# Gated products of the FFN made two units at a time on GpSimd, and the copies of unit 11 moved ahead of the exponentials

## What is computed

```python
x = x + conv(ln_c(x))                  # q, k, v, beta; the delta rule in chunks of 16 tokens; Wo
t = tokens(x)
h = ln_t(t)
g = silu(einsum('bsd,edh->bseh', h, w_gate))
u = einsum('bsd,edh->bseh', h, w_up)
routed = einsum('bse,bsed->bsd', top2(softmax(h @ router_w)), einsum('bseh,ehd->bsed', g * u, w_down))
shared = silu(h @ ws_gate) * (h @ ws_up) @ ws_down
t = t + alpha * shared + (1 - alpha) * routed      # alpha = sigmoid(h @ sg_w + sg_b)
```

## Time and profile before

| what | value |
|---|---|
| median of three runs | 483.0 us |
| the profiled execution's own time | 483.11 us |
| its span, first to last instruction | 481.4 us |
| busy: PE / DVE / POOL / ACT | 86% / 88% / 84% / 72% |
| POOL `hid` L1007 | 192 instructions, 112.8 us |
| POOL waiting for ACT's `ug` | 18.4 us in 18 waits |
| granted TensorE clock, mean | 0.947 |

### The profile page before, as it was taken

The page is one execution under the profiler, slowest core; times in us unless marked ns, Lnnn a source line. Parts: engine busy times, 40 slices in busy tenths (PEclk is TensorE's granted clock), DMA queues, the critical chain, the costliest instruction groups (busy, mean ns, idle before and its releaser), DMA issues.

```text
span 481.4 us, 10362 instructions
## 1 busy us (share of the span) xinstructions
PE 415.3 (86%) x2400; PEld 384.0 (80%) x2400; DVE 421.3 (88%) x2270; ACT 344.5 (72%) x997; POOL 406.0 (84%) x519
## 2 busy tenths in 40 slices
PE   1344446999999999999999999999999989899996
PEld 0233325898999989998999999999999979798895
DVE  4689969999999999999999999999999999996200
ACT  3699546586978786877878686969695847475862
POOL 4366978899999999999999999999999999986340
PEclk9976555999999999999999999999999999999999
DMA  6555672623242223222232322322323232200301
GB/s 164 161 124 131 155 184 73 167 73 98 66 109 81 91 68 89 73 87 78 81 89 72 98 77 84 93 82 81 89 75 90 78 95 84 90 1 1 115 2 16
DMA packets 43437, 42.91 MB, mean 89 GB/s; under 512 B 20144, under 2 KB 35184, under 8 KB 43376
## 3 DMA queue, kind: packets, MB, share of 16 engines
q1 hardware_dynamic: 42768, 42.05, 32.5%
q10 hardware_dynamic: 608, 0.21, 0.2%
HBM read 35.95 MB, written 6.29 MB: 88 GB/s over the span
## 4 chain that ended last, share of the span: by engine, by line
DVE 60%; POOL 10%; PE 10%; issue 7%; ACT 1%; POOLq 0%; DVEq 0%; ACTq 0%
DVE Pr L1423 13%; DVE bank L1427 13%; DVE u L1425 12%; DVE SH L1431 11%; POOL PQ L969 3%; POOL PQ L962 3%; PE bank L463 2%; POOL hid L1007 2%; DVE otok L1236 1%; PE bank L436 1%; PE bank L448 1%; DVE ss L1204 1%; PE bank L440 1%; PE bank L438 1%; PE bank L439 1%
## 5 line engine op out<-in xcount | busy, mean ns | idle before, releaser
L1007 POOL TENSOR_TENSOR hid<-sg,ug 128x192 f32<-128x192 f32 x192 | 112.8, 606 | 22.0 <-ACT ug L714 18.4
L962 POOL TENSOR_TENSOR PQ<-SH,QB 128x768 f32<-128x768 f32 x62 | 112.6, 1838 | 0.7 <-DVE SH L1431 0.7
L713 ACT ACTIVATE sg<-bank 128x192 f32<-128x192 f32 x192 | 64.3, 335 | 61.5 <-PE bank L440 48.7
L969 POOL TENSOR_TENSOR PQ<-PQ 128x768 f32<-128x768 f32 (+2 forms) x93 | 102.9, 1106 | 6.1
L463 PE MATMUL bank<-Wd,hidT 128*128 128x192 f32 x576 | 106.6, 326 | 0.0
L1427 DVE TENSOR_TENSOR bank<-bank,u 128x96 f32<-128x96 f32 (+1 forms) x467 | 104.5, 265 | 0.5
L1425 DVE TENSOR_REDUCE u<-Pr 128x6 f32<-128x102 f32 (+1 forms) x437 | 102.5, 268 | 0.8 <-issue 0.3
L1423 DVE TENSOR_TENSOR Pr<-SH,bank 128x96 f32<-128x96 f32 (+1 forms) x437 | 101.0, 265 | 1.4
L1431 DVE TENSOR_TENSOR SH<-SH,bank 128x96 f32<-128x96 f32 (+1 forms) x467 | 101.9, 255 | 0.3
L463 PEld LDWEIGHTS bank<-Wd,hidT 128*128 128x128 f32 x576 | 94.4, 190 | 0.0
L436 PE MATMUL bank<-Whi,hiT 128*128 128x384 f32 (+1 forms) x192 | 73.0, 380 | 1.1 <-DVE loT L1166 1.1
(11 more groups left out here) (143 smaller groups left out, 814.2 us busy)
## 6 DMA issues: line engine op xcount, KB each, us to landing
QB<-q_scratch SPq DMA_DIRECT2D x64, 384.0 KB
k_scratch<-khl SPq DMA_DIRECT2D x64, 48.0 KB, 1.7
KR<-k_scratch SPq DMA_DIRECT2D x32, 96.0 KB, 2.4
q_scratch<-qn SPq DMA_DIRECT2D x64, 24.0 KB, 1.9
Wd<-in_L_ffn_w_down_dram SPq DMA_DIRECT2D x4, 288.0 KB, 8.2
out_dram<-xT SPq DMA_DIRECT2D x1, 896.0 KB, 4.1
Wlo_unsplit<-in_L_ffn_w_gate_dram SPq DMA_DIRECT2D x2, 384.0 KB, 4.4
Wlo_unsplit<-in_L_ffn_w_up_dram SPq DMA_DIRECT2D x2, 384.0 KB, 5.9
```

What stands on the lines that cost most here:

```text
L962: tt(PQ[:, at * BR * HP:(at + n) * BR * HP].rearrange("p (i b h) d -> p i b (h d)", i=n, b=BR), SH[:, lo:lo + n].rearrange("p i b h d -> p ...
L969: chained(tt(PQ[:, :, 0:w], PQ[:, :, 0:w], PQ[:, :, w:2 * w], ALU.add))
L1007: tt(hid[:, r * H:(r + 1) * H], sg[:, m % RING], ug[:, m % RING], ALU.mult).then_inc(s_hid, 1)
```

## The change

GpSimd's `hidden(m)` now makes units m and m+1 in one instruction of 384 columns: it waits for the copies of both, and raises `s_hid` by 2 when both are done. The list of GpSimd calls it for m = 0, 2, 4, 6, 8, 10. The pair (10, 11) stands ahead of the first reading's sums; before, unit 11 stood behind them. The pair (6, 7) stands behind `rs`; before, unit 6 stood ahead of it. The pair (0, 1) of chunk c-1 stands behind the second reading, its sums and `vn`; before, unit 0 stood ahead of the second reading. On ScalarE unit 11 is copied behind the second group of `hidT`, ahead of the output's copies and the exponentials; before, it stood behind them. The waits of ACT and PE are unchanged.

```diff
 # ScalarE
                     at(-2, unit, 10)
                     at(-2, hidden, 1)
+                    at(-2, unit, 11)
                     at(-3, Fc_out)
                     table(c + 2, LN_EXP)
...
                     table(0, SILU)
                     at(-2, hidden, 2)
-                    at(-2, unit, 11)
                     at(-1, unit, 0)
 # GpSimd
             def hidden(q, p, m):
-                pool.wait_ge(s_ug, q * UN + (m + 1))
+                pool.wait_ge(s_ug, q * UN + (m + 2))
...
-                    last = ((m - UN // 2) % UN + 1) * H - 1
+                    last = ((m + 1 - UN // 2) % UN + 1) * H - 1
...
-                r = m % (UN // 2)
-                tt(hid[:, r * H:(r + 1) * H], sg[:, m % RING], ug[:, m % RING], ALU.mult).then_inc(s_hid, 1)
+                r, s = m % (UN // 2), m % RING
+                tt(hid[:, r * H:(r + 2) * H].rearrange("p (m h) -> p m h", m=2), sg[:, s:s + 2], ug[:, s:s + 2],
+                   ALU.mult).then_inc(s_hid, 2)
...
-                    at(-2, hidden, 6)
                     if c <= NC:
                         rsqrt(c)
-                    at(-2, hidden, 7)
+                    at(-2, hidden, 6)
                     once(c, 1, weights_1, 10)
                     once(c, 1, weights_1, 11)
                     at(0, reading, 0)
                     at(-2, hidden, 8)
-                    at(-2, hidden, 9)
                     at(-2, hidden, 10)
                     at(0, summing, 0)
                     at(2, A_kn)
-                    at(-2, hidden, 11)
                     at(2, A_qn)
-                    at(-1, hidden, 0)
                     at(0, reading, 1)
                     at(0, summing, 1)
                     at(2, A_vn)
-                    at(-1, hidden, 1)
+                    at(-1, hidden, 0)
                     at(-1, hidden, 2)
-                    at(-1, hidden, 3)
                     at(-1, hidden, 4)
-                    at(-1, hidden, 5)
                     at(2, A_klo)
```

## The result

The changed kernel takes **526.5 us**, the median of six runs (524.9 to 530.5), against 483.1 us of the kernel before beside it. The ratio is 1.091, with an interval of 1.089 to 1.093. The forecast was 513 us with a range of 505 to 522: the direction is right, and the time lies 4.5 us above the range.

A forecast was written before the change was run, and what follows sets the result against it. DVE's recurrence was taken to set the 25.18 us turn; the change closes a loop of 27.5 us, 13 x 2.32 = 30.2 us more, so 483.1 + 30.2 = 513.3, forecast 513 us, range 505 to 522.

The forecast's parts named there:

- The mechanism: Pair (0, 1) behind the second reading holds ACT's unit 4 copy, then PE and DVE, in every turn: 2.3 us a turn.
- the sign: Expected waits: ACT at unit 4 50 us in all, DVE at two st some 2 a turn, GpSimd for ug over 40.
- The loop: GpSimd from (6, 7) to (0, 1), back over ACT and PE: 27.5 us a turn against 25.18.
- The stretch on GpSimd: From the start of (6, 7) to the end of (0, 1), pairs, readings and sums without a gap: 20.73 us.
- The way back: Unit 4's copy, PE's units 6 to 7, unit 7's copy and four handovers: 6.75 us.
- no worse than now: GpSimd's rs standing ahead of pair (6, 7): claimed no worse than before, given no cost.
- 292.08 to 297.34: 5.26: PE from the start of unit 6 to the end of unit 7: 5.26 us, a term of the loop.
- I leave both out: Two last turns may pay some tenths less, the steps behind them some tenths more; neither counted.
- Unit 11: Early copy on ACT, 0.5 to 0.6 us ahead of prob: costed at nothing; without the hold up to 0.1 a turn.
- GpSimd as the bound: Rival: GpSimd sets the pace and six pairs save 0.9 us a turn, giving 469 us; chance 0.03.
- The absorbed hold: Rival: ACT's stop at unit 4 replaces existing waits, the turn stays 25.18 and the time about 483 us; chance 0.04.
- The dear pair: Rival: a merged GpSimd pair is no cheaper than two single products, giving 522 us; chance 0.15.

The follow-up runs named there:

- the kept clock's kernel: The changed kernel with fourteen extra matmuls, whose results nobody reads, ahead of unit 6 on PE in each repeating step: 518.4 us, ratio 1.073.
- the six-slot kernel: The changed kernel with six slots for sg and ug instead of four (RING = 6), nothing else: 490.0 us, ratio 1.015.
- the last experiment: The kernel before with only the pairs (4, 5) and (8, 9) merged: 482.5 us against 482.9, ratio 0.999.

## Why the prediction was right, and where it was wrong

**The mechanism was right.** ACT stops at unit 4 (57.5 us in 14 times; the sign named 50), DVE stops at the two `st` (32.4 us more in 13 turns, 2.5 each; the sign named 2), GpSimd has no gap from (6, 7) to (0, 1), and the run that moves unit 0 alone gives 516 us. GpSimd's waits at the pairs are larger than named: 21.1 us put down to `ug` and 49.7 us to "issue". In the turn above, 2.98 us of these end when ACT has copied unit 5 (at 351.81 to 352.22 on its timeline): a pair waits for its second copy there. At (6, 7), which the sign named too, the pair itself waits for 0.1 us in this turn, since `rs` ahead of it has waited.

**The loop was right at full clock.** The stretch on GpSimd was summed to 20.73 us and measured 20.80; the pair was taken at 1.0 us and measured 1.01. The way back was summed to 6.75 and measured 6.97: 0.1 on PE, which starts its first matmul behind a pause with 0.44 us, and 0.1 in the handovers. That `rs` makes this no longer is luck: the forecast called it "no worse than now" and did not follow its way back, which in the turn shown ends within 0.01 us of unit 7's. With the clock kept up, 13 turns take 27.68 us each against 27.5.

**The step that failed is the way back, "292.08 to 297.34: 5.26", as the price of every turn.** It was read in a turn of before in which PE had not paused. The same loop makes PE wait 1.7 to 1.9 us right ahead of unit 6, and in some turns PE then runs at 0.50 of its clock through just this part of the loop: 6.89 us instead of 5.36 in the slow turn shown, and 8.38 in the first of the 13, behind a pause of 3.36. The forecast named the pause (unit 6 three us late) and gave it no price beyond its length. Kept busy, the kernel is 8.2 us faster; so that is the missing term, and without it 518.4 lies in the range.

**A second, smaller one:** "I leave both out", of the last turns and the steps behind them. At kept clock they cost 2.7 us (35.1 us in all, of which 13 turns make 32.4). The account is then 513.3 + 13 x 0.18 (turns) + 2.7 (ends) + 8.2 (clock) = 526.5 us. That the sum closes is no further proof: the clock term is the difference of two measured kernels, and the ends are what the kept clock's kernel leaves over.

**Unit 11** was costed at nothing under the hold and at up to 0.1 us a turn without it. Without it it costs 4.1 us in all; the forecast looked at `sel`, where it is indeed 0.12 us a turn, and not at `hidT` behind the exponentials. Under the hold the forecast's zero was not tried by itself.

**The rivals.** GpSimd as the bound is excluded: the two cheapest pairs save work there and no time. The absorbed hold is excluded by ACT's 57.5 us and the turns. The dear pair is excluded by its 1.01 us. What none of the rivals said is that a pair costs by what it makes wait, at both ends: unit 0 waits for unit 1's copy (1.5 us in the turn read ahead of the reading, where the kernel, with the rest of the change, is 31 us slower than before), and unit 2 is ready 0.4 us later (2.1 us of the kernel).

**Open** is how the 6.8 us that the six-slot kernel keeps divide. The early unit 11 makes 4.1 us alone and the pair (2, 3) 2.1 alone, and they don't simply add. The six-slot kernel's ordinary turn is that of the early unit 11 alone, 25.75 us against 25.76, with the same delays in the same places, and nothing of the pair is seen in it; the run that takes unit 11 back has almost the same turn with the loss in another place. Where the rest lies was not found, and what six slots would do to the kernel before was not run.

## What to carry to other kernels

Before a producer is moved behind long work or merged with its neighbour, ask which slot it frees and who stands in order behind the one that waits for the slot; if the way leads back to the producer, the delay is paid in every turn, and a deeper ring is the cheap remedy (36.5 of 43.4 us here, for two slots). A merged instruction starts at its last input and gives its first output at its end, so only neighbours whose first consumer has room should be merged, and only on an engine whose time counts. Where an edit gives TensorE a new pause, price the work behind it at both clocks: 1.5 us here in a turn in which the clock fell for 3.4 us.

## What the runs showed of the hardware

The length of PE's pause alone does not tell whether the clock falls. In the changed kernel's profile PE waited 1.74 us ahead of unit 6 at 319.76 and the clock fell to 0.50 for 3.4 us; 1.74 us at 264.24 and at 292.00 and 1.89 us at 349.20 left it at 1.00, with the same matmuls around them. Behind the last turn PE waits 3.34 us for unit 4 and the clock is at 0.50 for 6.8 us; that lies where the profiled execution lost 5.2 us. Filling the pause kept the clock up: fourteen matmuls that nobody reads, 1.81 us long together, in idle time, made the kernel 8 us faster.

The mean clock of a run has to be read with care. The three shortest runs of the changed kernel (524.9 to 525.3 us) have a mean granted clock of 0.983 to 0.984, the three others (527.7 to 530.5) 0.928 to 0.938. But beside the last experiment the kernel before has two runs of 482.94 us at 0.931 and at 0.997: what a low clock costs depends on where in the kernel it falls.
